# Second-expert returns that begin with the seventh tile, six tiles kept in the join buffers, and the last 32 row transfers ahead of all returns

## What is computed

```python
x = L0_attn_x                                   # 32 x 256 x 128
xn = _layernorm(x)
x = x + linear_attention_with_elu(xn) + (top2_of_8_experts_silu(xn) + shared_expert(xn))
xn = _layernorm(x)
x = x + causal_gated_attention(xn)
      + top2_of_8_experts_gelu(xn)              # h = gelu(xn @ w1[e] + b1[e]); out = gate * (h @ w2[e] + b2[e])
```

## Time and profile before

| what | us |
| --- | --- |
| median of 3 runs | 920.0 |
| the runs | 923.14, 918.33, 920.0 |
| profiled execution, its own time | 914.01 |
| its span, first to last instruction | 912.3 |
| PE, DVE, ACT, POOL busy | 834.4, 700.9, 571.3, 621.0 |
| mean granted TensorE clock | 0.992 of full speed |

### The profile page before, as it was taken

One profiled execution on the slowest core, in us unless ns is written; L12 is line 12 of the kernel. 1 busy time (PEld: TensorE's weight loads), 2 busy tenths in 40 slices (PEclk: granted clock), 3 DMA queues, 4 the chain that ended last, 5 costly groups with the idle time before them and its releaser, 6 DMA issues.

```text
span 912.3 us, 22378 instructions
## 1 busy us (share of the span) xinstructions
PE 834.4 (91%) x7975; PEld 743.6 (82%) x7975; DVE 700.9 (77%) x1809; ACT 571.3 (63%) x1183; POOL 621.0 (68%) x598
## 2 busy tenths in 40 slices
PE   3789999999899999998898989887899799999997
PEld 3678878989799999985666666666899799999996
DVE  7787777886577998897899998898653565667776
ACT  5766465444476677769877786663755476566552
POOL 4156676777304788787888888887777777666663
PEclk9999999999999999999999999999999899999999
DMA  9799997115648999962111111116585777799996
GB/s 269 227 376 357 362 353 255 50 50 159 249 145 266 316 305 286 274 210 73 41 41 39 36 41 44 43 41 225 190 273 192 264 252 266 256 306 339 370 355 180
DMA packets 130990, 191.06 MB, mean 209 GB/s; under 512 B 15808, under 2 KB 85952, under 8 KB 130752
## 3 DMA queue, kind: packets, MB, share of 16 engines
q1 hardware_dynamic: 96720, 141.21, 47.0%
q0 software_dynamic: 16640, 34.37, 11.6%
q10 hardware_dynamic: 17520, 14.06, 4.9%
HBM read 110.74 MB, written 80.97 MB: 210 GB/s over the span
## 4 chain that ended last, share of the span: by engine, by line
PE 54%; DVE 23%; POOL 7%; issue 6%; ACT 4%; DMA 4%; SPq 0%; DVEq 0%; ACTq 0%; POOLq 0%
PE pair L910 12%; PE pair L856 5%; PE pair L857 5%; PE pair L887 5%; PE pair L858 5%; POOL sent L2046 5%; PE pair L690 3%; DVE a_en L1606 3%; PE pair L777 2%; DVE X L1539 2%; DVE stats_t L1168 2%; PE pair L697 1%; PE pair L698 1%; PE pair L699 1%; DVE X L1626 1%
## 5 line engine op out<-in xcount | busy, mean ns | idle before, releaser
L2046 POOL DMA_INDIRECT sent<-a_rows,slot x224 | 219.9, 982 | 78.4 <-issue 57.1
L2057 POOL DMA_INDIRECT ex_joined<-outs,slot x128 | 136.5, 1067 | 81.7 <-DMA outs<-ex_tile_out 45.4
L2148 POOL DMA_INDIRECT back<-ex_tile_out,address x136 | 150.4, 1106 | 60.7 <-issue 32.9
L856 PE MATMUL pair<-ex_x_hi,ex_w_hi 128*128 128x256 f32 x497 | 147.5, 297 | 0.1
L857 PE MATMUL pair<-ex_x_lo,ex_w_hi 128*128 128x256 f32 x497 | 141.3, 284 | 0.0
L858 PE MATMUL pair<-ex_x_hi,ex_w_lo 128*128 128x256 f32 x497 | 141.2, 284 | 0.0
L910 PE MATMUL pair<-ex_stage,ex_hid 128*128 128x128 f32 x1136 | 132.5, 275 | 0.0
L910 PEld LDWEIGHTS pair<-ex_stage,ex_hid 128*128 128x128 f32 x1136 | 129.9, 192 | 0.0
L1744 ACT ACTIVATE ex_w_hi<-ex_stage 128x768 fp32r<-128x768 f32 (+1 forms) x72 | 67.6, 938 | 90.5 <-DMA ex_stage<-in_experts 90.4
L1870 ACT ACTIVATE ex_hid<-pair,ex_stage 128x256 f32<-128x256 f32 x284 | 107.1, 498 | 0.1
L1377 DVE TENSOR_TENSOR ex_w_lo<-ex_stage,ex_w_hi 128x768 fp32r<-128x768 f32 (+1 forms) x72 | 77.4, 1075 | 25.5 <-ACT ex_w_hi L1744 25.1
(11 more groups left out here) (253 smaller groups left out, 2005.8 us busy)
## 6 DMA issues: line engine op xcount, KB each, us to landing
ex_stage<-in_experts SPq DMA_DIRECT2D x72, 578.0 KB
outs<-v_heads SPq DMA_DIRECT2D x8, 4352.0 KB, 36.8
ex_stage<-in_experts SPq DMA_DIRECT2D x72, 320.0 KB
ex_tile_in<-sent SPq DMA_DIRECT2D x72, 128.0 KB
outs<-ex_tile_out SPq DMA_DIRECT2D x71, 128.0 KB
ex_joined<-back ACTq DMA_DIRECT2D x15, 512.0 KB, 7.9
ex_tile_in<-sent SPq DMA_DIRECT2D x54, 132.0 KB
X<-in_x SPq DMA_DIRECT2D x16, 256.0 KB, 5.2
```

The costliest lines, as they stand in the source:

```text
L856: pe.matmul(o[:, of_half], wh, x_hi[i % 2][:, of_half], start=True, stop=False)
L2046: pool.indirect_dma_start(out=sent[layer], out_offset=bass.IndirectOffsetOnAxis(ap=slot_i[layer][k][:, s, j:j + 1], axis=0), in_=rows[laye ...
L2057: pool.indirect_dma_start(out=joined[g % NJOIN][:, j, k, :], out_offset=None, in_=outs, in_offset=bass.IndirectOffsetOnAxis(ap=slot_i[0][k ...
L2148: pool.indirect_dma_start(out=back, out_offset=bass.IndirectOffsetOnAxis(ap=address[i % NSIDE][:, s // HALF, s % HALF:s % HALF + 1], axis= ...
```

## The change

- The join buffers, free once group 15 is added, become the homes of the results of tiles 0 to 5 of the second expert stage (half a buffer each, `home`, `results_of`). The four buffers of `tile_out` serve tiles 6 and on, so `weigh1` waits for a return only from tile 10, again for that of tile n-4.
- All 32 row transfers of block 3 stand ahead of every return (`SENDS_LAST`), with no waits between them.
- The returns begin with tile 6. Their order is 6, 7, 8, 0, 9, 10, 1, 11, 2, 12, 3, 13, 4, 14, 5, 15, 16 and on (`BACK_ORDER`). Those of tiles 0 to 5 have no waits for PE.
- `EARLY` is 7: the first 12 tiles are the whole tiles of eight groups and need nothing of the last two blocks but what is in groups 0 to 7. The first join loads wait for tile 19 and stand a turn later (group 0 at turn 22); group 12's is at turn 34.
- In the attention the gathers of groups 11 to 15 stand in steps 3 to 9 (were 4 to 9), and steps 4 to 16 have six or seven transfers (were eight). Steps 17 to 20 hold the 32 of block 2.
- The arrays of `side` are parted: two for gates, 14 for addresses. So `side(n)` waits for the return of tile n-14, from n = 14 (was n-6, from 6).

```diff
-         {2: ((0, 0, 8),), 3: ((0, 8, 16),), 4: ((0, 16, 20),), 5: ((0, 20, 24),), 10: ((0, 24, 32),),
-          11: ((1, 0, 8),), 12: ((1, 8, 16),), 13: ((1, 16, 24),), 14: ((1, 24, 32),),
-          15: ((2, 0, 8),), 16: ((2, 8, 16),), 17: ((2, 16, 24),), 18: ((2, 24, 32),), 19: ((3, 0, 8),), 20: ((3, 8, 16),)})
-SENDS_LAST = {0: (3, 16, 24), 1: (3, 24, 27), 2: (3, 27, 30), 3: (3, 30, 32)}
-EARLY = 6
+         {2: ((0, 0, 8),), 6: ((0, 8, 12),), 9: ((0, 12, 15),), 10: ((0, 15, 22),), 11: ((0, 22, 29),), 12: ((0, 29, 32), (1, 0, 4)),
+          13: ((1, 4, 11),), 14: ((1, 11, 18),), 15: ((1, 18, 25),), 16: ((1, 25, 32),),
+          17: ((2, 0, 8),), 18: ((2, 8, 16),), 19: ((2, 16, 24),), 20: ((2, 24, 32),)})
+SENDS_LAST = (3, 0, 32)
+EARLY = 7
...
-NSTAGE, NIN, NOUT, NJOIN, NSIDE, AHEAD = (8, 4), 4, 4, 3, 6, 6
+NSTAGE, NIN, NOUT, NJOIN, NGATE, NADDRESS, AHEAD = (8, 4), 4, 4, 3, 2, 14, 6
+
+
+NEXTRA = 2 * NJOIN
...
-GATHERS = {4: ((11, 0, 4),), 5: ((11, 4, 8),), **{n - 6: ((n, 0, 8),) for n in range(12, 16)}}
-
-LAST_JOIN = {max(2 * g + 9, 2 * EARLY + 9 + g): g for g in range(14)}
+GATHERS = {3: ((11, 0, 8),), 4: ((12, 0, 7),), 5: ((12, 7, 8), (13, 0, 6)), 6: ((13, 6, 8),), 7: ((14, 0, 6),),
+           8: ((14, 6, 8), (15, 0, 4)), 9: ((15, 4, 8),)}
+
+LAST_JOIN = {max(2 * g + 9, 2 * EARLY + 8 + g): g for g in range(14)}
...
+FIRST_BACK = {8: 0, 10: 1, 11: 2, 12: 3, 13: 4, 14: 5}
+BACK_ORDER = [m for n in range(NEXTRA, LAST_BACK + 1) for m in ((n, FIRST_BACK[n]) if n in FIRST_BACK else (n,))]
...
+        def home(i):
+
+            n = i - NTILES
+            return NOUT + n if 0 <= n < NEXTRA else i % NOUT
+
+        def results_of(i):
+
+            h = home(i) - NOUT
+            if h < 0:
+                return tile_out[home(i)][:]
+            return joined[h // 2][:].rearrange("p s k c -> p (s k) c")[:, SUB * (h % 2):SUB * (h % 2 + 1), :]
+
         def results_dma(i):
-            return (put_dma, ret_dma)[i // NTILES][i % NOUT]
+            h = home(i) - NOUT
+            return (put_dma, ret_dma)[i // NTILES][home(i)] if h < 0 else join_half_dma[h // 2][h % 2]
...
-                if n >= NSIDE:
-                    j = i - NSIDE
+                if n >= NADDRESS:
+                    j = i - NADDRESS
                     dve.wait_ge(results_dma(j), returned(j))
...
-                dve.wait_ge(results_dma(i - NOUT), returned(i - NOUT))
+                if n >= NEXTRA + NOUT:
+                    dve.wait_ge(results_dma(i - NOUT), returned(i - NOUT))
...
-                    if s >= 1:
+                    if s >= 1 and n >= NEXTRA:
                         behind_tile1(n + 2, s - 1)
...
-            for n in range(NTILES):
-                if n in SENDS_LAST:
-                    s, first, end = SENDS_LAST[n]
-                    for i, jk in enumerate(range(first, end)):
-                        if n == 0:
-                            behind_tile1(i // NC1, i % NC1)
-                        else:
-                            behind_tile1(n + 1 + (i + 3) // NC1, (i + 3) % NC1)
-                        send(1, s, jk)
-                if n <= LAST_BACK:
-                    give_back(n)
+            s, first, end = SENDS_LAST
+            for jk in range(first, end):
+                send(1, s, jk)
+            for n in BACK_ORDER:
+                give_back(n)
```

More of the change, by code:

```diff
@@ L307, in build @@
         rms = sb("rms", [P, 2, 4, GT])
-        gate_t = [sb(f"gate_t{i}", [P, 4, 2, HALF]) for i in range(NSIDE)]
-        address = [sb(f"address{i}", [P, 2, HALF], I32) for i in range(NSIDE)]
+        gate_t = [sb(f"gate_t{i}", [P, 4, 2, HALF]) for i in range(NGATE)]
+        address = [sb(f"address{i}", [P, 2, HALF], I32) for i in range(NADDRESS)]
         sums_t = sb("sums_t", [P, 3 * P])
@@ L444, in build @@
         down_done, side_ready, out_ready = sem("down_done"), sem("side_ready"), sem("out_ready")
-        gathered_dma = [[sem(f"gathered_dma{i}{half}") for half in range(2)] for i in range(NJOIN)]
+        join_half_dma = [[sem(f"join_half_dma{i}{half}") for half in range(2)] for i in range(NJOIN)]
         joined_dma = [sem(f"joined_dma{i}") for i in range(NJOIN)]
@@ L494, in returns @@
             return halves(i) * (1 if i < NTILES else HALF)
+        def home(i):
[6 more added lines that the diff above has]
+            return joined[h // 2][:].rearrange("p s k c -> p (s k) c")[:, SUB * (h % 2):SUB * (h % 2 + 1), :]
         def results_dma(i):
-            return (put_dma, ret_dma)[i // NTILES][i % NOUT]
+            h = home(i) - NOUT
+            return (put_dma, ret_dma)[i // NTILES][home(i)] if h < 0 else join_half_dma[h // 2][h % 2]
         def returned(i):
-            return 16 * sum(returns(j) for j in range(i % NOUT, i + 1, NOUT) if j // NTILES == i // NTILES)
+            h = home(i) - NOUT
+            gathers = 0 if h < 0 else GT * len(range(h // 2, NG, NJOIN))
+            return 16 * (gathers + sum(returns(j) for j in range(i // NTILES * NTILES, i + 1) if home(j) == home(i)))
         def results_back(engine, i):
-            for j in range(i - NOUT + 1, i + 1):
+            for j in sorted({home(j): j for j in range(i // NTILES * NTILES, i + 1)}.values()):
                 engine.wait_ge(results_dma(j), returned(j))
@@ L923, in last_tokens @@
                         m = pe.matmul(bank[7][:, i * C:(i + 1) * C], is_of[:, SUB * (n - LAST_BACK - 1) + s, i * P:(i + 1) * P],
-                                      tile_out[(NTILES + n) % NOUT][:, s, :], start=(first and s == 0 and i == 0),
+                                      results_of(NTILES + n)[:, s, :], start=(first and s == 0 and i == 0),
                                       stop=(last and s == HALF * halves(n) - 1), skip_group_check=True)
@@ L1474, in side @@
                 r = tile_in[i // NTILES][i % NIN][:].rearrange("p (h s) c -> p h s c", h=2)
-                other, gate1, gate2, gate = (gate_t[i % NSIDE][:, k, :, :] for k in range(4))
+                other, gate1, gate2, gate = (gate_t[i % NGATE][:, k, :, :] for k in range(4))
                 mine = tile_first[:, 2 * n:2 * n + 2].unsqueeze(2).to_broadcast([P, 2, HALF])
                 dve.wait_ge(in_dma[i % NIN], 32 * (i // NIN + 1))
-                if n >= NSIDE:
-                    j = i - NSIDE
+                if n >= NADDRESS:
+                    j = i - NADDRESS
                     dve.wait_ge(results_dma(j), returned(j))
@@ L1484, in side @@
                 dve.tensor_tensor(gate, gate1, gate2, ALU.add)
-                dve.scalar_tensor_tensor(address[i % NSIDE][:], other, 0.0, r[:, :, :, TOK2], ALU.not_equal, ALU.add).then_inc(side_ready, 1)
+                dve.scalar_tensor_tensor(address[i % NADDRESS][:], other, 0.0, r[:, :, :, TOK2], ALU.not_equal, ALU.add).then_inc(side_ready, 1)
             def hidden0(n, c):
@@ L1533, in collect0 @@
             def collect0(g, half):
-                dve.wait_ge(gathered_dma[g % NJOIN][half], 16 * GT * (g // NJOIN + 1))
+                dve.wait_ge(join_half_dma[g % NJOIN][half], 16 * GT * (g // NJOIN + 1))
                 for k in range(K):
@@ L1877, in results0 @@
                 a = slice(0, SLOTS * halves(i))
-                act.activation(flat(tile_out[i % NOUT][:])[:, a], bank[7][:, a], ACT.Copy).then_inc(out_ready, 1)
+                act.activation(flat(results_of(i))[:, a], bank[7][:, a], ACT.Copy).then_inc(out_ready, 1)
             for n in range(NTILES + 1):
```

14 lines of the change are left out of this document (7 added, 7 removed).

## The result

The changed kernel takes 929.9 us (median of 4 runs, 926.19 to 930.6), the kernel before 919.63 in the same comparison (918.33 to 923.14): ratio 1.01, 95% interval 1.0056 to 1.0144. The forecast was 931.8, slower, by +11.8 us; measured are +10.3.

A forecast was written before the change was run, and what follows sets the result against it. PE sets the second expert stage's rhythm, its hole traced to POOL's one queue of transfers and returns. -8.8 + 14.3 + 6.6 + 1.3 + 1.4 - 3 = +11.8 us gives median 931.8, range 925 to 940 (8 in 10: 917 to 941).

The forecast's parts named there:

- gates of returns 9, 11, 13 and 15: Second expert stage: returns that weigh1 of tiles 15 to 18 needs, expected at 766.5, 777.2, 787.9 and 798.7 us.
- -8.8 + 14.3: Second expert stage: PE's hole closes, -8.8 us; late returns hold weigh1 up to tile 18, +14.3 us.
- spare of 1.1 us for tile 12: Second expert stage: tile 12's load expected ready at 718.2 us, PE wanting it at 719.3.
- the 8.8 us: PE's hole at tiles 9 and 10, closing credited to eight groups first; DVE's return wait made tile 5 1.5 us late.
- +6.6 for ACT's wait: Turn 22: ACT waits for tile 19's return, so rows come at 829.5 us against 822.9 wanted, +6.6 us.
- slower by more: Expert stage: returns at 5.67 us throughout, lower clock; sum +20, median 940; counted on the forecast's side, no separate chance.
- +1.3 for DVE's first join: Expert stage: DVE's first join finds its load late, 837.7 us against 836.4, +1.3 us.
- The end, +1.4: Kernel's end: joins of groups 11 and 12 both stand before the last group's load, one before; +1.4 us.
- Attention, -3: Layer-1 attention: some three meetings of POOL masks with DVE's joined-group adds go, 1 us each, -3 us.
- an attention more than 5 us shorter: Layer-1 attention: a sign that the prediction is wrong, if it ends more than 5 us earlier.
- POOL paces attention: Attention rival: 16 issues less give -20.3 us, median 914.5; chance 0.12 together with the other faster case.
- no change: Rival: POOL keeps its bare pace of 1.27 us, mean below 1.30; sum -1.6, measured 918.4; chance 0.13.

The follow-up runs named there:

- Run 5: Kernel before with only the tiles of eight groups first (EARLY 7) and joins from turn 22; ratio 1.0012, stage 235.1 us.
- Run 6: Changed kernel with the attention transfers and gathers, EARLY 6 and joins of the kernel before, and another return order; ratio 0.9873, 908.5 us.
- run 2: Changed kernel with 24 address buffers and the returns of tiles 0 to 5 put behind tile 19's; ratio 1.0127, stage 252.1 us.
- run 3: Changed kernel without the returns of tiles 0 to 5, their contribution missing from the output; ratio 0.989, stage 229.6 us.
- run 1: Changed kernel with 24 address buffers instead of 14; ratio 1.0065, stage 248.3 us.
- run 4: Kernel before with the changed attention's transfers and gathers alone, the 16 moved transfers ahead of tile 0's return; ratio 1.0142, stage 258.0 us.
- run 7: Kernel before, all transfers kept, with both POOL masks of an attention step one transfer earlier; ratio 0.9934.
- run 8: The edits of Run 6 and run 7 together: homes on the old attention, masks one transfer earlier; ratio 0.9827, 905.63 us.
- run 9: Kernel of Run 6 with nine transfers of steps 3 to 9 moved behind the last step, changed gathers and another return order; ratio 1.0006.
- run 10: Kernel of run 9 with both masks one transfer earlier in their step; ratio 1.0003.

## Why the prediction was right, and where it was not

*Right in sign and size, by its own chain.* POOL's queue is what sets the stage. The last transfer is issued at 711.3 us and all of them are through at 712.6 (forecast 710.7: 1.38 us each and not 1.35). The gates of returns 9, 11, 13 and 15 opened within 0.5 us of the times given. The first return is 1.9 us later than forecast, but a return takes 5.58 us up to the ninth and not 5.67, it can be used 3.5 us after the end of its gap and not 4.2, and between the first and the fourth gate a return takes (797.95 - 766.28) / 6 = 5.28 us and not 5.36. (The 4.2 were read from the end of an issue and added behind its gap of 0.30, so 0.3 of them were counted twice. And 43 issues stood ahead of the last row transfer before, not 44; nothing hangs on that.)

Part of this agreement is luck. The prediction expected all its times 3 us earlier in the profile, for the shorter attention (first return near 708). The attention became 6.6 us shorter, but everything ahead of it ran 5.5 us longer, and the stage began only 1.1 us earlier. Counted from the transposes of tile 2 the four gates are 0.9 to 1.6 us later than forecast.

*-8.8 + 14.3.* The changed stage lost 4.0 at tiles 12 and 13 and 13.1 at the returns, 17.1 in sum, where the forecast had no hole and 14.3. The spare of 1.1 us for tile 12 was used up: PE starts the stage 1.1 us earlier in this execution, and the transfers end 1.9 later. What PE loses there comes off the lateness behind it, so the two terms are off by 2.8 together and not by 4.

*The step that failed: whose gain the 8.8 us are.* The prediction gave 1.5 us of the hole to DVE's wait and the rest to tile 10's load, and the closing to the eight groups. Run 5 does just that and gains nothing: two more returns (tiles 2 and 3) were late in the kernel before, one at 706.19 and one at 715.46, and I had read only the waits ahead of the hole. Two causes lay side by side, and the 1.9 us of the slower tile behind them were counted with the load. Run 6 shows that the homes remove both without the eight groups. The sum didn't suffer, since the change has both parts.

*+6.6 for ACT's wait* measured 7.0, but only 4.7 of them come with the halt ahead of tile 25's transposes; run 2 and run 3 confirm its cause. The other 2.3 come in the tile behind it, run at a granted clock of 0.72, and the forecast had no term for that (its rival *slower by more* had one, 2 us). From tile 2 to tile 25 the forecast gives 178.9 us (23 tiles of 6.87, 14.3 and 6.6) and the profile 179.8. Behind it two misses cancel but for 1.2 us: the slower tile and 0.2 at tile 32 came unforeseen, and *+1.3 for DVE's first join* didn't come, because that join's load landed after 3.9 us (7.9 in the earlier trace rows is a median over all) and DVE's adds had no wait. *The end, +1.4*, measured +1.2: the last join load is 18.1 us behind tile 35 in the changed kernel and runs 1 to 3, 16.8 in runs 4, 6, 7 and 8; the difference of 1.3 is the join. (The kernel before has 17.4, and run 5, its kernel with the later joins, 18.7.)

*Attention, -3, measured -6.6.* The term was mis-sized, and its mechanism was only a part of it. The prediction named an attention more than 5 us shorter as a sign that it is wrong, and for this term it is; the total held because this miss of -3.6 and the stage's of +2.1 lie on opposite sides. I counted three meetings of a mask with the adds of a join. The masks also met `shift`, an instruction of 0.16 us that took 0.67 in the mean (the rows in run 7). Removing meetings alone brought 2.3 us of mask distance; the other 4.5 of 6.8 came with the fewer issues. With nine transfers fewer, the earlier masks brought nothing more (runs 9 and 10). The rival "POOL paces attention" thus looks less like a rival than like a second limit, just behind the first: 16 issues of 1.27 us fewer would give 20.3, and 6.8 arrived in all.

*Slower by more*, with returns at 5.67 us throughout, didn't occur; *no change* needed a mean issue below 1.30 us, and it was 1.38 over the 48 transfers and 1.37 over the 80 issues of the first 20 returns.

## What to carry to other kernels

Count a serial queue to its gates: the work moved behind a point, times its measured rate, against the first instruction that needs its end. Here 16 transfers gained 7 us where they left, and moving them alone lengthened the stage by 22.5 (run 4). A halt can also cost more than its own length: here the tile behind it ran slow for another 1.5 to 2.3 us. When a hole has a cause, look at the waits inside and behind it too before crediting its closing to one edit, because a second cause may be hidden under the first.

## What the runs showed of the hardware

A mask on POOL holds up DVE's instruction with two operands in SBUF, however small. In the kernel before:

```profile
483.51 1.56 DVE L1184 SCALAR_TENSOR_TENSOR shift<-moments,powers 128x4 f32<-128x4 f32 x1
```
```profile
483.95 1.10 POOL L2163 TENSOR_SCALAR_AFFINE_SELECT a_en<-a_en 128x1024 f32<-128x1024 f32 x1
```

The shift takes 0.16 us where no mask lies beside it; here it ends with the mask (485.07 and 485.05). Where a mask had begun first (526.68), the shift of 527.14 us took 0.67 and ended with it too (527.81 and 527.79). The Trainium skill (SBUF — State Buffer, "SBUF: two separate sides") calls the port pair of the two engines an exclusive lock held for a whole instruction. The end of the wait agrees. By the profile the shift started 0.44 us ahead of the mask, though, and the page gives the lock to whichever starts first; the record's start may not be the moment at which the port is asked for, and no run here settles that.

TensorE's clock falls around the longer halts. In eleven of the twelve profiles it is granted in full from the first to the last mask, and in kernels 6 and 8, where PE never halts from tile 2 to tile 35, over that stretch too. In the changed kernel PE's last halt, of 4.5 us, ends at 829.11, and the next tile takes 9.21 us at a mean clock of 0.72, part of it at the lower level (1.2 GHz), before 6.87 us at 1.00. Not every halt does this: in run 3 two of 1.1 and 1.2 us left the clock at 1.00.

Two things more. The distance between the first and the last mask repeats to 0.1 us over executions whose total differs by many, as long as the clock between them is 1.00 (run 7 is the exception), so a position inside a stage, read with the clock beside it, is a far finer measure than the time of the kernel. And of the five us that DVE had lost to masks, the attention got back 2.3.
